# A decoder's expert layer: its bias row added by two identity matmuls on TensorE, where GpSimd had added it to x

## The reference

```
base = x_norm @ W_base.T + b_base
gate = softmax(x_norm @ W_gate.T);  thr = sigmoid(x_norm @ W_thr + b_thr) * 0.125
w = max(gate - thr, 0), divided by its sum over the experts
moe = sum over experts of (x_norm @ A_e.T) * w_e @ B_e.T, times 2
x = x + base + moe
```

## Time and profile before

| | us |
|---|---|
| median of 3 runs | 960.92 (960.15 to 968.78) |
| the profiled execution | 966.79 |
| its span, first to last instruction | 965.0 |

### The profile page before, as it was taken

One profiled execution on the slowest core, in us unless ns is written; L12 is line 12 of the kernel. 1 busy time (PEld: TensorE's weight loads), 2 busy tenths in 40 slices (PEclk: granted clock), 3 DMA queues, 4 the chain that ended last, 5 costly groups with the idle time before them and its releaser, 6 DMA issues. The chain is left out here.

```text
span 965.0 us, 21225 instructions
## 1 busy us (share of the span) xinstructions
PE 899.9 (93%) x6504; PEld 465.1 (48%) x6504; DVE 781.6 (81%) x2090; ACT 636.2 (66%) x1787; POOL 662.4 (69%) x689
## 2 busy tenths in 40 slices
PE   4899999799999999999999999999769999999978
PEld 2355554344444554555555555545325555555543
DVE  6897887558867899899999999999658877677685
ACT  3788889644555676667766776676524588898561
POOL 5788888777775766766676676666338787675674
PEclk9899998799999999999999999999989997999999
DMA  9899999986555766665556556556526598987665
GB/s 358 177 175 164 180 173 184 177 175 122 97 87 133 126 135 113 120 129 112 124 124 127 107 125 130 112 119 131 110 64 155 132 149 148 152 154 130 116 159 144
DMA packets 384303, 136.32 MB, mean 141 GB/s; under 512 B 369760, under 2 KB 370400, under 8 KB 381792
## 3 DMA queue, kind: packets, MB, share of 16 engines
q1 hardware_dynamic: 384224, 135.39, 70.0%
HBM read 42.01 MB, written 2.10 MB: 46 GB/s over the span
## 5 line engine op out<-in xcount | busy, mean ns | idle before, releaser
L157 PE MATMUL bank<-w_hi,hT 128*128 128x512 f16 (+2 forms) x1024 | 320.0, 374 | 6.4 <-DVE hT L467 2.7
L157 PE MATMUL bank<-w_lo,hT 128*128 128x512 bf16 (+2 forms) x512 | 189.9, 373 | 0.0
L157 PE MATMUL bank<-w_hi,small 128*128 128x512 f16 x512 | 162.8, 379 | 7.8 <-DVE small L1567 7.8
L157 PEld LDWEIGHTS bank<-w_hi,hT 128*128 128x128 f16 (+1 forms) x1024 | 101.1, 100 | 109.9 <-issue 17.0
L1393 POOL TENSOR_TENSOR small<-small,mhalf 128x4 f32<-128x4 f32 x64 | 64.8, 1013 | 128.0 <-DVE small L974 128.0
L661 POOL TENSOR_TENSOR big<-big 128x512 f16<-128x512 f32 x96 | 111.4, 1169 | 27.0 <-DVE big L940 13.8
L1494 ACT ACTIVATE small<-small 128x128 f32<-128x128 f32 x256 | 98.7, 389 | 0.7 <-DVE small L1555 0.7
L157 PE MATMUL bank<-w_lo,small 128*128 128x512 bf16 x256 | 97.0, 379 | 0.0
L157 PE MATMUL bank<-small,big 128*128 128x17 f16 (+2 forms) x960 | 77.5, 213 | 9.4 <-DMA big<-big 6.5
L1409 POOL TENSOR_TENSOR w_lo<-stage,w_hi 128x512 bf16<-128x512 f32 x64 | 84.8, 1324 | 0.4 <-ACT w_hi L1530 0.4
L823 ACT ACTIVATE big<-bank,small 128x128 f32<-128x128 f32 x256 | 72.4, 381 | 17.3 <-DVE small L929 16.7
(11 more groups left out here) (210 smaller groups left out, 2110.0 us busy)
## 6 DMA issues: line engine op xcount, KB each, us to landing
stage<-in_weights SPq DMA_DIRECT2D x16, 1024.0 KB, 6.5
stage<-in_weights SPq DMA_DIRECT2D x64, 256.0 KB, 2.8
big<-big SPq DMA_TRANSPOSE x168, 3.3
small<-in_ctxT SPq DMA_DIRECT2D x2, 1024.0 KB, 12.0
big<-in_ctx SPq DMA_DIRECT2D x2, 1024.0 KB, 5.5
out<-x SPq DMA_DIRECT2D x8, 256.0 KB, 2.5
big<-in_vectors SPq DMA_DIRECT2D x5, 256.0 KB, 11.1
x<-in_x SPq DMA_DIRECT2D x2, 512.0 KB, 7.0
```

The lines of the kernel that those rows point to most:

```text
L157: last = nc.tensor.matmul(out, lhs(a, c), rhs(b, c), start=start and n == 0, stop=stop and n == 3 * chunks - 1)
```

## The change

The eight `x_bias` steps go. In their place `base_n` opens its bank with two matmuls, the fp16 identity times the hi half of the bias row and times its lo half, 512 columns each; the 12 matmuls of the base product then add to that. The row's halves and the identity must be ready before `base_0`: `eb_hi` on ACT now copies the identity to fp16 and the row to its hi half ahead of its own two instructions, and stands earlier on ACT, right behind `lxq_hi_1`. `eb_lo` on DVE now also makes the row's lo half, and stands earlier on DVE, between the two memsets `prep_0_0` and `prep_0_1`, ahead of `in_stats_5`. It waits for three of `eb_hi`'s instructions. `bq_lo` on POOL no longer copies the identity. `up_add` waits for x_bias no more, and the `p_hi` step waits for `e_lo` instead.

```diff
-        pe.wait_ge(self.bq_lo, 2)
+        pe.wait_ge(self.bq_lo, 1)
...
         if what == "base":
             self.rows_in.wait_turned(pe, n)
             after(pe, self.up_added, n - 1)
-            product(nc, self.Y[n % 2][:], tokens(chip, n), columns(chip.weight(self.base_slot)), CH, stop=False)
+            if n == 0:
+                pe.wait_ge(self.e_lo, 1)
+            nc.tensor.matmul(self.Y[n % 2][:], self.ident, self.row_split[0], start=True, stop=False)
+            nc.tensor.matmul(self.Y[n % 2][:], self.ident, self.row_split[1], start=False, stop=False)
+            product(nc, self.Y[n % 2][:], tokens(chip, n), columns(chip.weight(self.base_slot)), CH, start=False,
+                    stop=False)
...
         if what == "eb_hi":
             act.wait_ge(self.got, 64)
+            nc.scalar.activation(self.ident, chip.ident[:], ACT.Copy).then_inc(self.e_hi, 1)
+            nc.scalar.activation(self.row_split[0], self.brow, ACT.Copy).then_inc(self.e_hi, 1)
             nc.scalar.activation(self.b[0], self.bst, ACT.Copy).then_inc(self.e_hi, 1)
...
         if what == "eb_lo":
-            dve.wait_ge(self.e_hi, 1)
+            dve.wait_ge(self.e_hi, 3)
+            nc.vector.tensor_tensor(self.row_split[1], self.brow, self.row_split[0], ALU.subtract).then_inc(self.e_lo, 1)
             nc.vector.tensor_tensor(self.b[1], self.bst, self.b[0], ALU.subtract).then_inc(self.e_lo, 1)
...
-            nc.gpsimd.tensor_copy(self.ident, chip.ident[:]).then_inc(self.bq_lo, 1)
...
-        if what == "x_bias":
-            if n == 0:
-                pool.wait_ge(self.got, 64)
-            pool.wait_ge(self.rows_in.z_ready, n + 1)
-            at = slice(n * D, (n + 1) * D)
-            nc.gpsimd.tensor_tensor(chip.x[:, at], chip.x[:, at], self.brow, ALU.add).then_inc(self.x_bias, 1)
...
         if what == "up_add":
-            dve.wait_ge(self.x_bias, n + 1)
...
-        in_stats_4_0 in_z_3_0 prep_0_0 prep_0_1 in_stats_5_0 key_lo_1_0 in_z_4_0 in_stats_6_0 gates_take_0_0 in_z_5_0
+        in_stats_4_0 in_z_3_0 prep_0_0 eb_lo_0_0 prep_0_1 in_stats_5_0 key_lo_1_0 in_z_4_0 in_stats_6_0 gates_take_0_0 in_z_5_0
```

More of the change, by code:

```diff
@@ L937, in step @@
                 if begins(b) and n == 5:
-                    dve.wait_ge(opening.x_bias, NB)
+                    dve.wait_ge(opening.e_lo, 1)
                 rows_free(dve, n, b)
@@ L1708 @@
         in_stats_0_0 lxk_lo_0_0 in_stats_1_0 in_z_0_0 in_z_1_0 in_stats_2_0 in_stats_3_0 in_z_2_0 key_lo_0_0
-        in_stats_4_0 in_z_3_0 prep_0_0 prep_0_1 in_stats_5_0 key_lo_1_0 in_z_4_0 in_stats_6_0 gates_take_0_0 in_z_5_0
-        top_0_0 in_stats_7_0 share_0_0 eb_lo_0_0 in_z_6_0 key_lo_2_0 gates_take_1_0 share_lo_0_0 key_lo_3_0 up_add_0_0
+        in_stats_4_0 in_z_3_0 prep_0_0 eb_lo_0_0 prep_0_1 in_stats_5_0 key_lo_1_0 in_z_4_0 in_stats_6_0 gates_take_0_0 in_z_5_0
+        top_0_0 in_stats_7_0 share_0_0 in_z_6_0 key_lo_2_0 gates_take_1_0 share_lo_0_0 key_lo_3_0 up_add_0_0
         out_stats_0_0 prep_0_2 key_lo_4_0 top_1_0 gates_take_2_0 in_z_7_0 out_z_0_0 share_1_0 key_lo_5_0 top_2_0
@@ L1722 @@
     "scalar": """
-        lxk_hi_0_0 lxk_hi_1_0 lxq_hi_0_0 in_hi_0_0 in_hi_1_0 key_hi_0_0 in_hi_2_0 in_hi_3_0 lxq_hi_1_0 key_hi_1_0
-        key_hi_2_0 eb_hi_0_0 key_hi_3_0 in_hi_4_0 expo_0_0 bq_hi_0_0 in_hi_5_0 w_hi_0_0 share_hi_0_0 w_hi_1_0
+        lxk_hi_0_0 lxk_hi_1_0 lxq_hi_0_0 in_hi_0_0 in_hi_1_0 key_hi_0_0 in_hi_2_0 in_hi_3_0 lxq_hi_1_0 eb_hi_0_0 key_hi_1_0
+        key_hi_2_0 key_hi_3_0 in_hi_4_0 expo_0_0 bq_hi_0_0 in_hi_5_0 w_hi_0_0 share_hi_0_0 w_hi_1_0
         key_hi_4_0 in_hi_6_0 expo_1_0 out_hi_0_0 key_hi_5_0 in_hi_7_0 w_hi_2_0 w_hi_3_0 key_hi_6_0 key_hi_7_0
@@ L1733 @@
     "gpsimd": """
[L1734 to L1738, removed]
+        lxk_lo_pool_1_0 in_root_0_0 in_root_1_0 in_root_2_0 in_lo_0_0 in_root_3_0 in_lo_1_0 lxq_lo_0_0
+        in_lo_2_0 in_root_4_0 in_lo_3_0 in_root_5_0 lxq_lo_1_0 in_lo_4_0 in_root_6_0 in_lo_5_0
+        in_root_7_0 w_lo_0_0 w_lo_1_0 in_lo_6_0 out_root_0_0 out_lo_0_0 w_lo_2_0 w_lo_3_0 in_lo_7_0 out_root_1_0 q_lo_0_0 k_lo_0_0 ow_lo_0_0 q_lo_1_0 out_lo_1_0 v_lo_0_0
+        bq_lo_0_0 out_root_2_0 p_lo_0_0 v_lo_1_0 out_root_3_0 out_lo_2_0 q_lo_0_1 p_lo_2_0 q_lo_1_1
         p_lo_3_0 out_root_4_0 k_lo_0_1 out_lo_3_0 p_lo_5_0 ow_lo_1_0 out_lo_4_0 out_root_5_0 out_root_6_0 ow_lo_2_0
@@ L1778, in __init__ @@
         self.b = carve(late[:, L1_OUT], [(D, F16), (D, BF16)])
+        self.row_split = carve(late[:, L1_OUT.stop:L1_OUT.stop + D], [(D, F16), (D, BF16)])
         self.GB, self.Y, self.T = (chip.psum[1], chip.psum[7]), (chip.psum[6], chip.psum[5]), chip.psum[4]
@@ L1787, in __init__ @@
             sem(n) for n in ("gated", "gates_taken", "chain", "expo", "shared", "share_turned", "share_hi", "share_lo"))
-        self.y_done, self.x_bias, self.up_added = sem("y_done"), sem("x_bias"), sem("up_added")
+        self.y_done, self.up_added = sem("y_done"), sem("up_added")
         self.wide_done, self.wide_hi, self.wide_lo = sem("wide_done"), sem("wide_hi"), sem("wide_lo")
@@ L1923, in tensor @@
             if n == 0:
-                pe.wait_ge(self.e_lo, 1)
+                pe.wait_ge(self.e_lo, 2)
             pe.wait_ge(self.s_lo, n // 2 + 1)
```

## The result

| | us |
|---|---|
| changed, median of 16 runs | 968.87 (963.28 to 971.73) |
| before, median of 16 runs | 962.04 (959.04 to 968.78) |
| ratio | 1.005, 95% interval 1.0031 to 1.0068 |
| changed, the profiled execution | 965.6, of which 963.8 span |

The changed kernel is slower by 0.5%, 4.8 us, by the interval 3.0 to 6.5 us. The two medians lie 6.8 us apart, just outside that interval; this text goes by the ratio.

What follows compares the result with a forecast made beforehand. The prediction took POOL and DVE to bound the kernel before 731.58 us, then PE. Terms 0.76 + 1.73 + 0.4 gave +2.9 us, from a median of 960.92 to 963.8; own range 962.4 to 965.9, stated range 958 to 969.

Steps and rivals of the forecast that it cites:

- Step 1: Sixteen new 512-column matmuls on PE, in eight base steps, at 0.216 us each: 3.46 us.
- Step 2: x_bias_0 leaves POOL, where it ran beside in_z_1 on DVE: gates_1 could begin 1.09 us earlier.
- Rival A: x_bias_0 was not what held in_z_1, so the start gains nothing: +4.0, 964.9 us; chance 0.11.
- Step 3: eb_hi and eb_lo moved forward delay in_stats_5, lxq_lo_1 and load_0; up_0 begins at 743.45 us: +0.76 instead of -0.23.
- Step 4: base_2 to base_5, ahead of up_5 on PE: 8 of the 16 matmuls, all on the chain, 1.73 us.
- Step 5: base_6 and base_7, where DVE, ACT and POOL alternate with PE: half of 0.86 us counted, 0.4.
- Step 6: PE's clock around gates_1 and up_0, where idle times change: taken as 0.
- the second alternative: A new half-clock stretch follows PE's new idle time before up_0: +1.6 us, but taken as 0.
- The first alternative: The 3.2 us at half clock go, freeing 1.6 us of PE time, which the wait for load_0 takes: 0.
- rival B: PE's clock stays up from 794.3 to 804.7 us, saving at most 5.1 us: 958.7 us; chance 0.10.
- sign of being wrong: The forecast is wrong if load_0 lands as before, in_z_1 still takes 1.6 us, or PEclk dips change in number or length.
- Rival C: PE's clock falls more often, at up_0 and the first self-attention steps: +9.6, 970.5 us; chance 0.09.

Runs made afterwards that it cites:

- before_again: Kernel before, unedited, second profiled execution: 72.90 us from ACT's first instruction of the second half to the start of up_add_7.
- before_third: Kernel before, unedited, third profiled execution: 72.92 us from ACT's first instruction of the second half to the start of up_add_7.
- before_fourth: Kernel before, unedited, fourth profiled execution: 72.77 us from ACT's first instruction of the second half to the start of up_add_7.
- no_matmuls: Changed kernel without its sixteen identity matmuls, so the bias row is left out of the output: 964.29 us, ratio to before 1.0013.
- double: Changed kernel with each pair of identity matmuls issued twice, so the bias row counts double: 971.63 us, ratio to before 1.0093.
- split_later: Changed kernel with eb_lo moved on DVE from ahead of in_stats_5 to behind in_z_4: 965.05 us, ratio to before 1.0024.
- bias_later: Kernel before with x_bias_0, x_bias_1 and x_bias_2 moved on POOL to behind in_root_7: 963.64 us, ratio to before 1.001.
- bias_spread: Kernel before with x_bias_0 behind in_root_7 on POOL, x_bias_1 and x_bias_2 ahead of x_bias_3: 969.55 us, ratio to before 1.0083.
- bias_shift: Kernel before with each of the first five x_bias steps one place later on POOL: 963.06 us, ratio to before 0.9983.

## Why the forecast was right in kind and too small in size

The steps have the numbers that they have in the prediction.

**Step 1, the price of a matmul: right.** New and old matmuls start 0.21 to 0.22 us apart (730.88, 731.10, 731.31 us), and E moves by 2.3 to 2.6 us for twelve of them.

**Step 2, x_bias_0 beside in_z_1: right.** in_z_0 and in_z_1 together take 1.17 us in after and 2.24 to 2.25 in before_again, before_third and before_fourth, and gates_1 starts 0.8 to 1.1 us earlier in every kernel that has no x_bias_0 there, with the matmuls and without (0.8 where it follows gates_0 without a wait). Rival A falls, by its own test. By the rule of the Trainium skill ("SBUF — State Buffer", section "Who interferes with whom") the first to start holds the port; the traces do not agree for this pair, since in all four executions of before in_z_1 is recorded 0.08 us ahead of x_bias_0 and was the one that lost 1.1 us. Nor do they for in_z_4 and lxq_lo_1 after: in_z_4 is recorded 0.02 us ahead (727.28 and 727.30 us) and takes 2.42 us. An in_z step has one tensor in SBUF as input, not two, so these pairs may lie outside the rule as the prediction cites it.

**Step 3, eb_lo ahead of in_stats_5: the places are right, the size of the loss is the term that failed.** On the scale of before in_stats_5 ends at 730.75 us (forecast 730.9), lxq_lo_1 starts at 731.35 (731.4) and up_0 at 743.25 (743.45). Of the two things that could hold up_0, the later load and the later share_0, the second won: the prediction names it as leading to the same 743.5 us, with share_0 and share_turn_0 near 740.7, and share_turn_0 starts at 740.37. The load path is close behind: share_lo_0 ends 0.15 us before up_0 starts. Two of the prediction's signs therefore did not come as written: PE's new idle time is not before up_0, and ACT waits no longer for load_0 (3.18 us, against 3.10 in the earlier trace rows), since ACT itself comes to it later.

What failed is the sum made of it: "a sum of -0.23 becomes +0.76". Both numbers are differences from up_0 at 742.69 us, and that lies 1.65 us late, since the execution that was read had PE at half clock from 733.0 to 736.2 us. The three executions of before without the dip have up_0 at +29.3, the three of the changed kernel without one at +31.5 to +31.8: the step costs 2.2 to 2.5 us, not 0.76. The prediction saw the dip and argued that the later load would swallow what its going frees. It was swallowed, by the later share_0, but then the difference holds against this one execution alone. Against it the forecast is nearly exact: the second half takes 256.13 us after, 253.28 before, +2.85. That is partly luck: up_0 comes 0.56 us later (forecast 0.76), from there to up_add_7 it is 2.66 (forecast 2.13), and the part behind, where nothing was forecast, gives back 0.4. The sum was then carried over to a median of executions that, as far as four profiled ones tell, mostly have no dip, and there 1.2 to 1.3 us were missing (74.10 less 72.86 in E).

**Step 4, base_2 to base_5: right.** up_add_5, which takes up_5's bank, starts at 775.45 us after and 777.15 before, 2.35 us later by the common scale; the forecast is 2.5. From up_0 to there it is 1.8 us, against the forecast 1.73.

**Step 5, base_6 and base_7: too small, by 0.4 us.** They fall where the engines alternate, but E carries all twelve later matmuls.

**Step 6, the clock: the second alternative, in one execution of four.** It was priced at +1.6; it moves up_0 by 1.5 to 1.7 and E by 1.2 us (78.60 less 77.36). As a term it should have been a share of that rather than 0. The first alternative, that the dip behind gates_1 goes, holds in all four executions after, and frees nothing in the three of before that have no such dip.

**The sum.** From dip-free execution to dip-free execution E goes from 72.86 to 77.36, +4.5 us: 2.2 up to share_turn_0, and 2.3 from twelve matmuls. The timed differences follow E over all seven kernels. By the ratios, against before, they are +5.5 us for the changed kernel (E +4.5), +1.3 for no_matmuls (+1.9), +9.0 for double (+6.8), +2.3 for split_later (+2.0), +1.0 for bias_later (+0.8), +8.0 for bias_spread (+7.5) and -1.6 for bias_shift (+0.2), and each E lies within its interval.

Behind up_add_7 some of it seems to come back: the rest of the span is 179.4 us on average before and 178.5 after. Two of the four executions of before have PE at a mean clock of 0.77 from 790 to 812 us, where the other two have 0.95 and 0.99 and the four after 0.97 to 1.00. So the second dip of rival B is missing after. But the two executions of before with that dip have a rest of 179.2 and 179.9 us, the two without it 178.7 and 179.9: its going saves nothing that can be seen, far from the 5.1 us of rival B. No run here shows that the change caused its absence. The prediction's sign of being wrong, dips that change in number or length, came about, but they change as much between executions of one kernel, so this sign could not tell. Rival C, a clock that falls more often on the whole, does not show.

**Why the gain at in_z_1 bought nothing.** bias_later shows that it is worth 1.1 us at gates_1, and bias_shift 0.9 at up_0; in both the moved additions lengthen DVE steps elsewhere, share steps above all, and by up_add_7 nothing of it is left. In the changed kernel nothing of it arrives, since share_0 on DVE is the next thing late; with eb_lo moved back (split_later) it pays for the four matmuls of base_0 and base_1.

## What to carry to other kernels

A forecast made against one profiled execution holds for that execution: when it contains a stretch that others may not have (here 3.2 us at half clock behind an idle time), work out the sum with and without it, or profile the kernel a second time. Where a step is moved forward on an in-order engine, price the wait it brings and not its own length: eb_lo's 1.3 us of work stood in front of in_stats_5 with 3.11 us of waiting for ACT, and moving it back by four places took half of the loss away. And work taken off POOL was a gain here only where it had run beside a DVE step on the path; before moving such work elsewhere, look at what DVE does there.

## What had not been expected of the hardware

- A DVE step of a few columns can lose as much to a POOL instruction as one of 512 columns. The share step of 2 columns (L2043, L2044) takes 0.16 us alone. It takes 1.12 beside in_lo_5 (POOL 734.16 to 735.31, the step 734.21 to 735.33), 1.20 beside an addition (751.80 to 753.07, the step 751.89 to 753.09) and 2.11 beside a w_lo split: each time it began just behind the POOL instruction and ended with it. So the price is what is left of the POOL instruction, whatever the step's own length. These pairs agree with the first-to-start rule of the Trainium skill cited above; in_z_1 and, after, in_z_4 are the pairs that do not. Every in_z step that lost time beside POOL in the fourteen traces (95 steps of 0.6 us or more) ended 0.28 to 0.29 us after a POOL instruction. Not every small step pays: in before_third a RECIPROCAL of 4 columns at 755.52 us, beside in_lo_7 (POOL 755.42 to 756.58), takes 0.18 us, as long as with POOL idle.
- The clock does not answer to the same idle time in the same way. Behind idle times of PE of 2.07 to 2.29 us before share_turn_0 it fell to 0.50 in one of four executions, and in no_matmuls it did not fall behind 2.87 us there. Before gates_1 there was a fall behind 1.96 us and none behind 0.31 to 0.93.
- The unchanged first half ends anywhere between 706.3 and 712.6 us in these profiles, a spread larger than the whole effect; only the count from a common instruction made the traces comparable.
